# Batch 0's first norm inside attention's last steps, and batch 0 ahead of batch 1 up to the quantiser

## Chip, cores and metric

The kernel runs on one core of a Trainium2 chip. The metric is the device time of one execution in microseconds (us). Before the change it is 2540.73 us, the median of 3 runs (2538.59 to 2546.09).

## What is computed

Eight sequences of 512 tokens with 256 channels go through four layers. Cut to what matters here:

```
h = attention(x)                                  # 16 heads of 16, softmax, projection w_out
h = concat([cls_tok, h], axis=1)                  # T = 513 tokens
n = layernorm(layernorm(h)) * ln_w + ln_b         # the first norm, taken twice in a row
a = sigmoid(n @ W_alpha.T + b);  u = n @ W_B.T + b
s[t] = a[t] * s[t-1] + u[t]                       # recurrence over the tokens
h = h + s @ W_C.T + b + D * layernorm(h)
h = h + ffn0(layernorm(h))                        # the second norm; bit_linear: per token max,
                                                  # round(x * 127 / max), ternary weights;
                                                  # conv over 3 tokens; silu; bit_linear
h = h + mamba(layernorm(h));  h = h + ffn1(layernorm(h))
```

The two norms of the first layer share one variance: two roots, of (1+eps) var + eps^2 and of var + eps, give both scalings.

## The kernel before, in words

Activations lie with channels on partitions and tokens along the free dimension, 256 channels as two tiles of 128 x 513. A pair of sequences ("batch 0" and "batch 1", `p` = 0, 1) is worked at a time; four turns cover the eight. Each of the engines TensorE (PE), ScalarE (ACT), VectorE (DVE) and GpSimd (POOL) has its own instruction stream, written out by hand in the order of issue, and waits on counting semaphores; SyncE (SP) issues the DMAs. Nothing is reordered between streams by a planner.

**Attention** runs in 37 steps (`STEPS`), a head of either batch each. In step s TensorE makes four score tiles ("units", which rotate through PSUM banks 0 to 2 in the order of `plan_units`, and of which VectorE frees one at a time), four to six "shifted" score tiles of a head 8 steps back (L890), whose exponentials ScalarE takes (two tiles, 1024 columns, per activation, L1197), and at fixed steps the values product of a group of four heads (L902). A group's outputs are copied and shuffled (L1728, L1730), their sums inverted by ScalarE with Ln and Exp (`invert_sums`), and normalised by VectorE (L1737 to L1743) or GpSimd. Batch 0's projection stands in steps 29 and 30 (`O_STEP`), batch 1's behind the last step (L909), its last quarter behind four dummy matmuls (L762).

**Between attention and the first FFN** both batches go through each step together: `layer_norm(0)` (mean on TensorE by a matmul with 1/256, subtraction on VectorE L1577, square on ScalarE, variance on TensorE, Ln and Exp on ScalarE, product on VectorE L1583 and L1587), the affine on ScalarE, gates and inputs of the recurrence (weights `wa`, `wB`, L755), the scan on VectorE (L1786), its output product (`wC`), the residual (L1792, L1797), `layer_norm(2)`, the maximum over channels (`absmax`, L1591), per token maxima by transposes (L805, L1614), the scale spread as two rows "I" and "S" (L818), and the quantiser (L1644, L1524). ScalarE holds one table set at a time: Ln with Exp, Sigmoid, or Silu; a switch is an instruction of its own (L1201, L1300, L1317).

**The first FFN** is a loop over 2 x 8 tiles of 128 hidden channels: a fill on TensorE (L755), the scale by VectorE (L1813) or by ScalarE's copy and GpSimd (L2096), the convolution over tokens on TensorE for tiles 1, 2, 4 and 7 (L774) or as three taps on ScalarE and VectorE (L1819, L1825) for the others, Silu, and VectorE's maxima (L1596).

From the first norm on, every product of TensorE takes one of four PSUM slots in turn, in the order of `plan_fills`; a product waits until the reader of the slot's last content is done (`readers`). So the order of fills is also an order of waits. The functions are these:

## Time and profile before

| | |
|---|---|
| median of 3 runs | 2540.73 us |
| profiled execution | 2544.26 us, of which span 2542.4 us |
| turns | 4 |
| mean granted TensorE clock | 0.946 of full |

The profile is of one execution. PE's busy time is that of its matmuls, PEld's that of its weight loads, which overlap them. "x" counts instructions; a float32 matmul shows as two records. A line number is that of the kernel before; a helper's line (L755 for every fill, L1197 for every activation) is shared by many uses, so tile names and times tell them apart. In the timeline, instructions of one kind in a row are merged: the start is of the first, the us from the first start to the last end.

### The profile page before, as it was taken

The page shows a single profiled execution, that of the slowest core. Times are in us where ns is not written, and L with a number is a line of the kernel's source. Part 1 is how long each engine was busy: PE and PEld are TensorE (multiplying, and loading weights), DVE is VectorE, ACT ScalarE, POOL GpSimd, SP SyncE. Part 2 cuts the span into 40 slices and gives each one's busy share as a digit, 9 for nine tenths or more (in the row PEclk, how much of TensorE's full clock was granted, in tenths as well). Part 3 has the DMA queues.
Part 4 walks back from the last instruction along what each step waited for, and adds up shares of the span by engine and source line. Part 5 has one row for each costly group of instructions (what it writes and reads, how often), then busy time and mean ns, then how long its engine had stood idle before and what let it go on. Part 6 is the DMA issues. An engine that isn't in the chain of part 4 may idle for free.

```text
span 2542.4 us, 26885 instructions
## 1 busy us (share of the span) xinstructions
PE 2142.9 (84%) x9366; PEld 1193.9 (47%) x9366; DVE 2029.6 (80%) x2434; ACT 1488.5 (59%) x2363; POOL 1120.8 (44%) x562
## 2 busy tenths in 40 slices
PE   3998878897799887989779898788978988878897
PEld 1326664345423765434542476543553246644445
DVE  6865879997785588998788477999788747799977
ACT  2654468765275447875537544787453644577744
POOL 1220249982222115997222111799522311279952
PEclk8999999999899998999899998899989999889998
DMA  6200000000220000000031000000003100000000
GB/s 202 84 6 1 1 1 1 1 1 1 83 77 1 1 1 0 1 1 1 1 109 51 1 1 1 1 0 1 1 13 112 36 1 1 1 1 0 1 1 17
DMA packets 41087, 51.45 MB, mean 20 GB/s; under 512 B 9072, under 2 KB 32368, under 8 KB 40944
## 3 DMA queue, kind: packets, MB, share of 16 engines
q1 hardware_dynamic: 40944, 49.62, 6.3%
q8 instruction: 80, 1.31, 0.2%
q14 instruction: 63, 0.52, 0.1%
HBM read 26.25 MB, written 10.49 MB: 14 GB/s over the span
## 4 chain that ended last, share of the span: by engine, by line
DVE 40%; PE 39%; ACT 9%; issue 8%; POOL 3%; DMA 1%; SPq 1%; DVEq 0%; ACTq 0%; POOLq 0%
DVE big L1983 16%; PE psum L755 11%; PE psum L902 5%; ACT big L1197 4%; PE psum L818 3%; ACT mid L1197 3%; PE psum L890 3%; PE psum L875 3%; PE psum L1057 3%; DVE big L1652 2%; PE psum L1089 2%; POOL big L2132 2%; DVE mid L1596 2%; DVE negmax L1704 2%; DVE mid L1524 2%
## 5 line engine op out<-in xcount | busy, mean ns | idle before, releaser
L1197 ACT ACTIVATE big<-psum 128x512 f32<-128x512 f32 (+2 forms) x604 | 455.8, 774 | 277.3 <-PE psum L890 146.8
L2132 POOL TENSOR_TENSOR big<-big 128x2048 f32<-128x2048 f32 x124 | 561.8, 4530 | 41.3 <-DVE big L1983 41.2
L1057 PE MATMUL psum<-big,ident 128*128 128x512 f32 x992 | 507.0, 617 | 65.6 <-POOL big L2132 65.6
L1983 DVE TENSOR_TENSOR_SCAN big<-psum,b,big 128x512 f32<-128x512 f32 x404 | 490.2, 1265 | 6.9 <-ACT psum L1197 6.6
L1704 DVE TENSOR_REDUCE negmax<-psum 128x1 f32<-128x512 f32 x512 | 318.7, 678 | 47.2 <-PE psum L875 46.1
L1197 ACT ACTIVATE psum<-mid,aneg 128x512 f32<-128x512 f32 x404 | 268.5, 680 | 80.2 <-DVE big L1983 80.1
L1057 PEld LDWEIGHTS psum<-big,ident 128*128 128x128 f32 x992 | 174.4, 193 | 230.9 <-POOL big L2132 141.3
L875 PE MATMUL psum<-mid 96*128 96x512 bf16 x512 | 189.0, 389 | 49.3 <-DMA mid<-mid 38.1
L890 PE MATMUL psum<-mid 98*128 98x512 bf16 x512 | 182.2, 382 | 20.1 <-ACT big L1197 14.3
L1197 ACT ACTIVATE mid<-mid 128x513 f32<-128x513 f32 (+3 forms) x120 | 104.3, 883 | 154.7 <-DVE mid L1993 80.6
L2096 POOL TENSOR_TENSOR big<-big,mid 128x513 f32<-128x513 f32 x40 | 50.8, 1282 | 286.3 <-ACT big L1197 286.3
L2121 POOL TENSOR_TENSOR big<-mid,big 128x512 f32<-128x512 f32 (+1 forms) x128 | 154.8, 1209 | 19.9 <-ACT big L1197 19.9
L1197 ACT ACTIVATE mid<-psum 128x513 f32<-128x513 f32 (+1 forms) x100 | 59.3, 597 | 170.2 <-PE psum L818 139.3
L1927 DVE TENSOR_TENSOR big<-mid,psum 128x1024 f32<-128x1024 f32 (+1 forms) x128 | 157.5, 1230 | 0.1
L818 PE MATMUL psum<-ident,tok 128*128 128x128 f32 (+1 forms) x640 | 120.4, 340 | 33.3 <-DVE tok L1631 15.4
L902 PE MATMUL psum<-big,mid 128*32 128x512 f32 x1024 | 135.0, 627 | 10.6 <-ACT osb L1197 10.6
L1031 PE MATMUL psum<-bcp,sel 96*128 96x512 bf16 x256 | 101.8, 404 | 47.1 <-DVE big L1983 22.7
L1075 PEld LDWEIGHTS psum<-big 128*128 128x128 f32 x864 | 114.1, 193 | 57.7 <-issue 51.4
L1983 DVE TENSOR_TENSOR_SCAN big<-big,b,psum 128x512 f32<-128x512 f32 x108 | 135.6, 1256 | 3.9 <-ACT psum L1197 2.1
L1197 ACT ACTIVATE big<-ident,big 128x128 f32<-128x128 f32 x432 | 136.4, 386 | 0.0
L818 PEld LDWEIGHTS psum<-ident,tok 128*128 128x128 f32 (+1 forms) x640 | 108.8, 246 | 53.5 <-DVE tok L1631 21.1
L875 PEld LDWEIGHTS psum<-mid 96*128 96x128 bf16 x512 | 49.8, 98 | 178.0 <-DVE negmax L1704 85.1
(224 smaller groups left out, 3837.5 us busy)
## 6 DMA issues: line engine op xcount, KB each, us to landing
mid<-mid SPq DMA_DIRECT2D x192, 64.0 KB, 2.6
mid<-scratch SPq DMA_DIRECT2D x192, 64.0 KB, 2.2
scratch<-big SPq DMA_DIRECT2D x4, 1536.0 KB, 6.1
out<-hres SPq DMA_DIRECT2D x8, 513.0 KB, 5.0
big<-in_x SPq DMA_DIRECT2D x8, 512.0 KB, 5.5
big<-in_w SPq DMA_DIRECT2D x2, 1024.0 KB, 6.4
big<-in_wg SPq DMA_DIRECT2D x1, 1024.0 KB, 9.7
big<-in_wu SPq DMA_DIRECT2D x1, 1024.0 KB, 11.6
```

Source lines behind the costliest of these rows:

```text
L755: mm = nc.tensor.matmul(o[:, a:b], lhs, rhs[:, a:b], start=(n == 0), stop=(n == len(products) - 1))
L818: mm = nc.tensor.matmul(o[:, t0:t0 + n], tok[0:n, p, which, c:c + 1].broadcast_to([n, P]), ident[0:n, 0:n], start=True, stop=True)
L875: nc.tensor.matmul(unit(("S", h, t)), q_stack[0:ROWS_MAX, h % H, t * P:(t + 1) * P], k_stack[0:ROWS_MAX, h % H, :], start=True, stop=True) ...
L890: mm = nc.tensor.matmul(st_unit(v)[:, t % 2], k_stack[0:KROWS, h % H, t * P:(t + 1) * P], q_stack[0:KROWS, h % H, :], start=True, stop=True)
L902: mm = nc.tensor.matmul(pv_bank[32 * j:32 * j + 32, :], vaug[:, g // NG, t, HG * (g % NG) + j], probs[:, g % 2, j, t], start=(t == 0), sto ...
L1057: mm = nc.tensor.matmul(y_psum[:, c], ident[:, :], st(1, k)[:, c], start=(n == 0), stop=(n == NS - 1))
L1197: return nc.scalar.activation(o, a, func, **kw)
L1704: V.tensor_reduce(negmax[:, m % 2, k:k + 1], unit(("S", h, t)), AX_X, ALU.max, negate=True).then_inc(unit_free, 1)
L1927: V.tensor_tensor(st(0, k)[:, 0:m], mid4(k // NS, 3)[:, 0:m, 1:T], b_psum.unsqueeze(1).broadcast_to([P, m, S]), ALU.mult).then_inc(b_used, 1)
L1983: V.tensor_tensor_scan(st(0, k)[:, c], decays(DT * k + c), bx, b0[:, p, n, c:c + 1], ALU.mult, ALU.add).then_inc(scanned, 1)
L2121: G.tensor_tensor(st(0, k)[:, m:b_end(k)], mid4(k // NS, 3)[:, m:b_end(k), 1:T], b_row(k).unsqueeze(1).broadcast_to([P, b_end(k) - m, S]), ...
L2132: G.tensor_tensor(st(1, k), st(0, k), c_row(k).unsqueeze(1).broadcast_to([P, DT, S]), ALU.mult).then_inc(hc_ready, 1)
```

## The change

Batch 0's first norm moves into attention: mean behind step 31, square behind 32, variance behind 33, both roots behind 34, products behind 35, affine behind 36. Its mean and variance are taken in two halves of 257 and 256 tokens, as units in the banks of the scores. Batch 0's two gate fills come ahead of the last quarter of batch 1's projection, in place of the four dummy matmuls. From there batch 0 goes first through recurrence, second norm, maxima, token rows and quantiser, with batch 1's steps between them (`LRU_ORDER`), and batch 1's variance, transposes, token rows and quantiser stand inside the loop over FFN tiles (`AMONG`, `AT_R2`, `AT_N2`, `AT_T0`, `AT_I0`). The dummy matmuls ahead of the gates and ahead of the first transposes are gone. Two more switches of ScalarE's table set are made. The stacks of queries and keys lie group by group, and batch 0's norm writes over groups whose heads are done. The later norms' functions are only split up; their order is as before.

```
-WARM = {"affine": 20, "T0": 12, "I1_0": 10, "T1_1": 14, "I1_1": 6, "LN3": 8, "T2": 4, "T3_1": 14, "I3_1": 6}
-WARM_O = 4
+WARM = {"I1_0": 10, "T1_1": 14, "I1_1": 6, "LN3": 8, "T2": 4, "T3_1": 14, "I3_1": 6}
...
+LRU_ORDER = [("a0", 0), ("a1", 0), ("mean0", 1), ("u0", 0), ("u1", 0), ("var0", 1), ("c0", 0), ("c1", 0), ("a0", 1),
+             ("a1", 1), ("u0", 1), ("mean2", 0), ("u1", 1), ("var2", 0), ("c0", 1), ("c1", 1), ("T0", 0), ("I0", 0),
+             ("S0", 0), ("mean2", 1)]
+AMONG = {1: (("var2", 1),), 4: (("T0", 1),), 5: (("I0", 1), ("S0", 1))}
+AT_R2, AT_N2, AT_T0, AT_I0 = 2, 3, 5, 6
...
+MEAN_STEP, SQUARE_STEP, VAR_STEP, RSTD_STEP, NORM_STEP, AFFINE_STEP = (O_STEP + n for n in (2, 3, 4, 5, 6, 7))
...
+        if s == MEAN_STEP:
+            u.extend(("mean", n) for n in range(2))
+        if s == VAR_STEP:
+            u.extend(("var", n) for n in range(2))
...
-        q_stack = mb[:, 0:H * S].rearrange("p (h q) -> p h q", h=H)
-        k_stack = mb[:, H * S:2 * H * S].rearrange("p (h q) -> p h q", h=H)
+        stacks = mb[:, 0:2 * H * S].rearrange("p (j s h q) -> p j s h q", j=NG, s=2, h=HG)
...
+                def halves(key, stream):
+                    for n, (a, b) in enumerate(HALVES):
+                        unit_ready((key, n))
+                        for k in range(KT):
+                            mm = nc.tensor.matmul(unit((key, n))[:, 0:b - a], mean_w[:, :], stream[:, k, a:b],
+                                                  start=(k == 0), stop=(k == KT - 1))
+                        mm.then_inc(unit_full, 1)
...
+                    if s == MEAN_STEP:
+                        pe.wait_ge(cls_ready, 1)
+                        pe.wait_ge(unit_free, UNITS["O", 0, 1] + 1)
+                        halves("mean", hres[:, 0])
+                    if s == VAR_STEP:
+                        pe.wait_ge(squared0[0], 1)
+                        halves("var", mid2(0, 1))
...
-                        keep_busy(psum[:, spare * BANK:(spare + 1) * BANK], WARM_O)
+                        pe.wait_ge(probs_ready, 2 * HG * NGRP)
+                        pe.wait_ge(affine, KT)
+                        recurrence_inputs("a", wa, 0)
...
+                pe.wait_ge(cls_ready, PAIR)
+                mean(0, 1)
+                recurrence_inputs("u", wB, 0)
+                variance(0, 1)
+                recurrence_outputs(0)
+                pe.wait_ge(affine, 2 * KT)
+                recurrence_inputs("a", wa, 1)
+                recurrence_input("u0", wB, 1)
+                pe.wait_ge(h1_ready, KT)
+                mean(2, 0)
+                recurrence_input("u1", wB, 1)
+                variance(2, 0)
+                recurrence_outputs(1)
+                token_maxima(0, (0,))
+                token_rows(0, (0,))
+                pe.wait_ge(h1_ready, 2 * KT)
+                mean(2, 1)
                 for s in range(PAIR * HT + CONV_LAG):
+                    for part, b in AMONG.get(s, ()):
+                        if part[0] == "v":
+                            variance(2, b)
+                        elif part[0] == "T":
+                            token_maxima(0, (b,))
+                        elif part[0] == "I":
+                            token_rows(0, (b,))
...
+                def both_roots_first():
+                    one, two = mid1(0, 4), mid1(0, 5)
+                    for n, (a, b) in enumerate(HALVES):
+                        act.wait_ge(unit_full, UNITS["var", n] + 1)
+                        o = unit(("var", n))[:, 0:b - a]
+                        run(one[:, a:b], o, ACT.Ln, scale=1.0 + EPS, bias=eps_sq[:, 0:1]).then_inc(rstd0[0], 1)
+                        run(two[:, a:b], o, ACT.Ln, bias=eps[:, 0:1]).then_inc(unit_free, 1)
+                    act.wait_ge(rstd0[0], 2)
+                    run(one, one, ACT.Exp, scale=-0.5).then_inc(rstd0[0], 1)
+                    act.wait_ge(unit_free, UNITS["var", 1] + 1)
+                    run(two, two, ACT.Exp, scale=-0.5).then_inc(rstd0[0], 1)
+                def both_roots_second():
+                    wait_full(act, "var0", 1)
+                    for n, kw in enumerate((dict(scale=1.0 + EPS, bias=eps_sq[:, 0:1]), dict(bias=eps[:, 0:1]))):
+                        row = mid1(1, 14 + n)
+                        run(row, slot("var0", 1), ACT.Ln, **kw).then_inc(rstd0[1], 1)
+                        act.wait_ge(rstd0[1], 2 * n + 1)
+                        run(row, row, ACT.Exp, scale=-0.5).then_inc(rstd0[1], 1)
...
+                    if s == SQUARE_STEP:
+                        act.wait_ge(unit_free, UNITS["mean", 1] + 1)
+                        run(mid2(0, 1), mid2(0, 0), ACT.Square).then_inc(squared0[0], 1)
+                    if s == RSTD_STEP:
+                        both_roots_first()
+                    if s == AFFINE_STEP:
+                        affine_part(0)
                 invert_sums(NGRP - 1)
-                layer_norm(0)
                 nc.scalar.preload_act_table(ACT.Sigmoid)
-                for p in range(PAIR):
-                    act.wait_ge(ln_normed, q_of(0, p))
-                    for c in range(KT):
-                        run(mid2(p, 1)[:, c], mid2(p, 1)[:, c], ACT.Identity, bias=col("lnb", c),
-                                      scale=col("lnw", c)).then_inc(affine, 1)
                 act.wait_ge(pads, 4)
-                for p in range(PAIR):
-                    for c in range(KT):
-                        wait_full(act, f"a{c}", p)
-                        run(mid2(p, 3)[:, c, 1:T], slot(f"a{c}", p)[:, 1:T], ACT.Sigmoid, bias=col("ba", c)).then_inc(
-                            alpha_ready, 1)
-                    for c in range(KT):
-                        wait_full(act, f"u{c}", p)
-                        run(mid2(p, 4)[:, c], slot(f"u{c}", p), ACT.Identity, bias=col("bB", c)).then_inc(u_ready, 1)
+                gates(0)
                 load_ln_exp()
-                layer_norm(2)
-                nc.scalar.preload_act_table(ACT.Silu)
-                copy_rows(0)
+                act.wait_ge(centered0, 1)
+                run(mid2(1, 2), mid2(1, 0), ACT.Square).then_inc(squared0[1], 1)
+                for c in range(KT):
+                    gate_input(0, c)
+                both_roots_second()
+                nc.scalar.preload_act_table(ACT.Sigmoid)
+                affine_part(1)
+                gates(1)
+                load_ln_exp()
+                gate_input(1, 0)
+                squares(2, 0)
+                gate_input(1, 1)
+                log_variance(2, 0)
+                inverse_root(2, 0)
+                copy_rows(0, (0,))
+                squares(2, 1)
                 for s in range(PAIR * HT + 5):
+                    if s == AT_R2:
+                        log_variance(2, 1)
+                        inverse_root(2, 1)
+                        nc.scalar.preload_act_table(ACT.Silu)
+                    if s == AT_I0:
+                        copy_rows(0, (1,))
...
+                def normalise_first(p):
+                    dve.wait_ge(rstd0[p], 2 if p else 3)
+                    V.tensor_tensor(mid2(p, 1), mid2(p, 0), over_channels(mid1(p, 14 if p else 4)), ALU.mult).then_inc(
+                        normed0[p], 1)
+                    dve.wait_ge(rstd0[p], 4)
+                    V.tensor_tensor(mid2(p, 0), mid2(p, 0), over_channels(mid1(p, 15 if p else 5)), ALU.mult).then_inc(
+                        normed0[p], 1)
+                def centre_halves():
+                    for n, (a, b) in enumerate(HALVES):
+                        dve.wait_ge(unit_full, UNITS["mean", n] + 1)
+                        V.tensor_tensor(mid2(0, 0)[:, :, a:b], hres[:, 0, :, a:b],
+                                        unit(("mean", n))[:, 0:b - a].unsqueeze(1).broadcast_to([P, KT, b - a]),
+                                        ALU.subtract).then_inc(unit_free, 1)
...
+                    if s == MEAN_STEP:
+                        centre_halves()
+                    if s == NORM_STEP:
+                        normalise_first(0)
...
+                centre(0, 1)
+                recurrence(0)
+                normalise_first(1)
+                add_recurrence(0)
+                centre(2, 0)
+                recurrence(1)
+                norm_maxima(2, 0)
+                scales(0, 0)
+                add_recurrence(1)
+                quantise(0, 0, mid2(0, 0), mid2(0, 2), mid_bf(0, 1, 2))
+                centre(2, 1)
                 for s in range(PAIR * HT + 4):
+                    if s == AT_N2:
+                        norm_maxima(2, 1)
+                    if s == AT_T0:
+                        scales(0, 1)
+                    if s == AT_I0 + 1:
+                        quantise(0, 1, mid2(1, 0), mid2(1, 2), mid_bf(1, 1, 2))
```

## Rows read from the trace of the kernel before

**Rows 1.** The page, part 1: busy us (share of the span) and instructions.
```profile
PE 2142.9 (84%) x9366; PEld 1193.9 (47%) x9366; DVE 2029.6 (80%) x2434; ACT 1488.5 (59%) x2363; POOL 1120.8 (44%) x562
```
**Rows 2.** Windows, the FFN stage of turn 2: busy of each engine, clock, DMA.
```profile
875.00:917.00 42.00, 36.05 (x196) 28.76 (x194) 37.70 (x35) 22.27 (x37) 15.40 (x11) 0.96 0.00 1
```
**Rows 3.** Chain of waits, turn 2: start us, us, what.
```profile
814.33 2.01 PE psum L755 x8
...
816.36 1.24 DVE mid L1577
...
866.12 8.48 PE psum L818 x40
```
**Rows 4.** Timeline of TensorE, turn 2: start, us, line, shapes, [idle before <-releaser].
```profile
787.30 0.59 PE L890 MATMUL psum<-mid 98*128 98x512 bf16 x2 [0.55 <-ACT big L1197]
...
793.53 5.34 PE L902 MATMUL psum<-big,mid 128*32 128x512 f32 x32
...
802.78 3.64 PE L902 MATMUL psum<-big,mid 128*32 128x512 f32 x32
...
811.50 1.98 PE L909 MATMUL psum<-big,wo 128*128 128x512 f32 x4 [0.59 <-DVE big L1743]
...
843.26 7.09 PE L755 MATMUL psum<-mid,wC 128*128 128x257 f32 x32
...
874.53 2.57 PE L755 MATMUL psum<-mid,w 128*128 128x257 bf16 x20
877.56 2.83 PE L774 MATMUL psum<-big,onorm 128*128 128x257 f32 x12 [0.46 <-issue]
...
886.75 1.48 PE L755 MATMUL psum<-mid,w 128*128 128x257 bf16 x12
```
**Rows 5.** Timeline of VectorE, turn 2.
```profile
844.25 2.29 DVE L1786 TENSOR_TENSOR_SCAN mid<-mid 128x1026 f32<-128x1026 f32 x1 [4.63 <-ACT mid L1197]
846.47 1.39 DVE L1792 SCALAR_TENSOR_TENSOR hres<-psum,vec,hres 128x513 f32<-128x513 f32 x2
...
864.77 0.68 DVE L1614 TENSOR_REDUCE tok<-psum 128x4 f32<-128x512 f32 x1
...
875.14 0.70 DVE L1524 TENSOR_SCALAR mid<-mid 128x1026 bf16<-128x1026 f32 x1
...
887.46 0.69 DVE L1813 TENSOR_TENSOR big<-psum,mid 128x513 f32<-128x513 f32 x1 [0.62 <-PE psum L755]
```
**Rows 6.** Timeline of ScalarE, turn 2.
```profile
789.88 3.77 ACT L1197 ACTIVATE big<-psum 128x1024 f32<-128x1024 f32 x4 [1.80 <-PE psum L902]
...
820.77 0.69 ACT L1197 ACTIVATE mid<-psum,eps_sq 128x513 f32<-128x513 f32 x1 [0.36 <-PE psum L755]
...
825.27 1.15 ACT L1197 ACTIVATE mid<-mid 128x513 f32<-128x513 f32 x2
826.44 1.28 ACT L1300 ACT_TABLE_LOAD   x1
827.74 2.93 ACT L1197 ACTIVATE mid<-mid,vec 128x513 f32<-128x513 f32 x4
...
970.72 0.30 ACT L1197 ACTIVATE big<-psum 128x128 f32<-128x128 f32 x1
```
**Rows 7.** Windows of TensorE, turn 2: us, busy (records), granted clock, DMA share, GB/s.
```profile
790.00:793.00 3.00, 1.60 (x7) 1.00 0.01 1
793.50:797.00 3.50, 3.50 (x21) 0.56 0.00 0
909.00:912.00 3.00, 0.00 (x0) 1.00 0.00 0
914.00:920.00 6.00, 6.00 (x20) 0.50 0.01 3
```
**Rows 8.** Timeline of TensorE, token rows of turns 1 and 4.
```profile
243.96 5.65 PE L818 MATMUL psum<-ident,tok 128*128 128x128 f32 x40 [0.44 <-DVE tok L1631]
...
2115.57 9.95 PE L818 MATMUL psum<-ident,tok 128*128 128x128 f32 x40 [0.29 <-DVE tok L1631]
```

More of the change, by code:

```diff
@@ L132, in plan_fills @@
         order.extend((None, None, ("v0", p), ("v1", p)))
-    ln(0)
-    each("a0", "a1", "u0", "u1")
-    each("c0", "c1")
-    ln(2)
-    quantiser(0)
+    order.extend((None, None))
+    order.extend(LRU_ORDER)
     for s in range(PAIR * HT + CONV_LAG):
+        order.extend(AMONG.get(s, ()))
         if s < PAIR * HT:
@@ L1130, in mean4 @@
                     pe.wait_ge(h3_ready, 3 * p + 3)
[L1131 to L1135 removed]
+                    mean(4, p)
                 def project_last(c):
@@ new lines, in both_roots_second, with affine_part @@
+                def both_roots_second():
[5 more added lines that the diff above has]
+                        run(row, row, ACT.Exp, scale=-0.5).then_inc(rstd0[1], 1)
+                def affine_part(p):
+                    act.wait_ge(normed0[p], 1)
+                    for c in range(KT):
+                        run(mid2(p, 1)[:, c], mid2(p, 1)[:, c], ACT.Identity, bias=col("lnb", c),
+                            scale=col("lnw", c)).then_inc(affine, 1)
@@ L1257, in turn_functions, with gates, gate_input @@
+                def gates(p):
+                    for c in range(KT):
+                        wait_full(act, f"a{c}", p)
+                        run(mid2(p, 3)[:, c, 1:T], slot(f"a{c}", p)[:, 1:T], ACT.Sigmoid, bias=col("ba", c)).then_inc(
+                            alpha_ready, 1)
+                def gate_input(p, c):
+                    wait_full(act, f"u{c}", p)
+                    run(mid2(p, 4)[:, c], slot(f"u{c}", p), ACT.Identity, bias=col("bB", c)).then_inc(u_ready, 1)
                 copy_high(1)
```

222 lines of the change are left out of this document (98 added, 124 removed).

## Prediction

> **What bounds the kernel now.** I read the page first: VectorE is busy 80% of the span, TensorE 84%; neither is full, so hand-overs decide [rows 1]. The four turns are alike and I work in the second. Its windows say that the FFN stage is VectorE's, 37.70 of 42 us [rows 2]. The chain of waits before that stage goes through the mean, the centring, and on to 8.48 us of token rows: one engine at a time [rows 3]. So I read what the change is worth at one instant, the start of batch 1's first FFN fill, 886.75 (the first of three fills that the row merges, rows 4). VectorE takes it at 887.46 [rows 5] and is nearly full from there; all work behind it is the same in the same order, so a shift here reaches the end.
>
> **First stretch: attention's last steps.** Batch 0's norm goes between heads that TensorE and ScalarE already share.
> TensorE: a product of 8 records costs 1.73 us (7.09 us for 32, less the last's drain of 0.15, over four, rows 4). The mean starts at 786.60, where TensorE would idle to 787.30 [rows 4], and ends at 788.33, 1.03 us late. The values behind it and so ScalarE's next exponential move from 789.88 to 790.91 [rows 6]; the DMA of the last maxima moves as much and lands before it is wanted. The square is as wide as one of the four exponentials in that row (3.77 / 4, some 1.0 with its end); behind two of them it ends at 793.81. The variance runs 793.87 to 795.60, and the next heads' values start at 796.13 instead of 793.53: 2.60 late.
> Now a gain. These 32 value records took 5.34 us and the next 32 took 3.64 [rows 4]. The clock was granted at 0.56 during the first, after a stretch with TensorE busy 1.60 of 3 us [rows 7]. Mean and variance fill that hole; I take the fast price, 1.70 less, delay 0.90. If the clock still falls, that gain is nil.
> ScalarE takes both roots between two exponentials. Four Ln of about 257 columns have no row: from above 0.69, a Ln of 513; from below 0.30, an activation of 128 [rows 6]; between them by columns 0.43, or 0.38 in a row. Two Exp (1.15 for two, rows 6, and a wait of each on its input) make it 2.58. The last exponential is 3.49 late, the last values 3.09 (they had waited for a projection): 805.87 to 809.44, two projections to 813.08.
> Then both gate fills, 3.46 us, stand ahead of the last projection. It used to wait until 811.50, 5.1 behind the values [rows 4], for VectorE's copy, ScalarE's Ln and Exp and three steps more; now that is ready at 814.53, so 1.45 of 3.46 are covered. It starts at 816.54. **First term +5.04 us.** The affine (two of 2.93 / 4, rows 6) lies in ScalarE's wait for the last sums: nothing, 1.5 without that cover. GpSimd's taps start as much later and are wanted only by the first convolution: nothing. The new layout of the stacks moves the same bytes in as many DMAs: nothing, bounds 0.5 us either way.
>
> **Second stretch: to batch 1's scan.** The residual that the mean at 814.33 [rows 3] read is ready at 819.32. Mean 2.01 to its reader [rows 3]; behind it batch 0's input fills, 3.46; variance full at 826.60. ScalarE's four (0.69 and about 0.65 each) end at 829.22, the sigmoid load of 1.28 [rows 6] at 830.52, the affine at 832.04. Two gate fills and an input fill, batch 0's second mean at 837.29, the last input fill, full at 841.08. ScalarE has batch 0's square ahead of it and copies it by 842.26; scan 842.33 to 844.62. Before, it ended at 846.54 [rows 5]. **Second term −6.96**: 1.92 ahead, batch 0's recurrence and both its norms done beside it. Here the change gains.
>
> **Third stretch: to batch 1's maxima.** Now batch 0 stands in front. Behind the scan VectorE normalises batch 0 (1.24, as the centring, rows 3), takes its maxima (as long), waits for two fills and the transposes to 848.85, takes the scales (0.68 of reduction [rows 5] and four small ones, 1.35 to where the token rows start at 866.12 [rows 3], 0.2 for the last) and adds batch 1's recurrence only at 850.35 (two pairs of 1.39, rows 5, overlapping): 853.06, against 852.46. Mean, centring, square and variance: full at 859.60. ScalarE has an FFN copy ahead of Ln and Exp (861.76), then the Silu load (863.1), another copy and tile 0's product (864.4). VectorE has tile 0's tap queued ahead of the normalisation, and it waits for that product: tap to 865.2, normalisation 866.4, maxima 867.60. Before, maxima ended at 864.77 [rows 5]. **Third term +4.75**: 2.83 late.
>
> **Fourth stretch: to batch 1's first fill.** Before, 864.77 to 886.75 is 21.98 us, mostly both batches' token rows and batch 0's fills and convolutions. After, TensorE is idle from 860.7 to 867.65, and then has in its queue: batch 1's transposes (0.7), fill f4 (2.57 / 5), convolution 1 (2.83), batch 1's token rows (half of 5.65 at full clock, rows 4 and 8), fill f5. At full clock f5 is full at 874.95. ScalarE then copies f5, makes a product and a Silu, copies both rows, and reads convolution 1 (six of some 0.57, 3.4 us); only that read frees the PSUM slot that convolution 2 wants, at 878.5. **This is the new wait that I expect to rule.** Queued behind it are f6 and, on VectorE behind f6 (0.69) and a tap, batch 1's quantiser (1.24 and 0.70, rows 3 and 5): convolution 2 to 881.3, first fill of batch 1 at 885.1, 1.65 early.
> But the clock will not hold. After 3 us of idleness to 912 it was at 0.50 from 914 to 920, TensorE busy all the while [rows 7]; here the idleness is 7 us. A low spell between 3.5 and 6.8 us (the token rows of turn 4 ran cold over nearly all of 9.95, those of turn 1 in 5.65, rows 8) costs half its length, 1.7 to 3.4. A second is due at convolution 2, behind 3.7 us of idleness: 0.4 to 2.5 (5.3 for 2.8). First fill 887.2 to 891.0; I take 889.1. **Fourth term −0.48**, and the sum is +2.35.
> The other old turns are shorter by 0.36 on average, last projection to first fill, as their token rows ran from 5.65 to 9.95 [rows 8] against 8.48. So +2.7 a turn, **+10.8 us** in four. The profiled execution took 2544.26 us: 2555.1. The median of the runs is 3.53 lower: 2551.5, rounded down.
>
> **A rule against the change.** The rows: a table load took 1.28 us; it began 0.02 after the end of the activation before it, and the one behind it began 0.02 after its own end [rows 6]. The change makes five loads a turn of three. Two newly lie on the path, for sigmoid and for Silu, both in the terms; one has left it.
> The Trainium skill (ScalarE: Activation LUTs, "What ACT_TABLE_LOAD costs") adds to the load of about 1.28 us a drain of about 1.38 at every switch, and asks to do all of one set before the next. By that rule the estimate would be 1.4 us a turn more. These rows show no drain.
>
> **Rivals.**
> *The clock holds* (22%). TensorE stays at 1.00 through the queue behind batch 1's transposes. For: the token rows of turn 1 took 5.65 us after a pause of 2.25. Against: the pause is 7 us. It decides below 886.4 in the second turn, where the mean old turn stands. Price 885.1 − 886.4 = −1.3 a turn, −5 in all: 2535.5; with Ln at its lower bound (4 × 0.13 less) and the layout's 0.5 gained −2.3, 2531.5. This is the side of faster.
> *The first term is smaller* (12%): the affine and both roots fit where ScalarE waits for TensorE, 2.6 us less a turn: 2541.
> *Cold throughout* (13%): group 6's values stay slow (+1.7), batch 0's own rows run cold (2.8 more at most, 1.4 likely) and the spells are long (+1.9 less what overlaps): +3 a turn over mine, 2563.
> *A load drains* (3%): both on the path twice as long, by rows 2 × 1.28 × 4 = 10 more: 2561.
>
> **How the numbers follow.** My forecast has 50%, and its own range is 2544 to 2558. A measurement can tell about 0.3% from no change, 7.6 us: 2533.1 to 2548.3. Of my case 31% lies inside. Slower: 0.69 × 50 and 16, some 50%. Same: 0.31 × 50, 12 and 4 of the clock's case, 32%. Faster: its other 18. The range, 2533 to 2565, takes in most of the clock's case below and the cold one above.
>
> **What would show it.** Right: in turn 2, 28 us from the first shifts of step 32 to the last projection (24.2 before); 28 from there to the end of batch 1's scan (35 before); an idle TensorE of 6 to 7 us ahead of batch 1's transposes, and of 3 to 4 ahead of convolution 2, released by ScalarE; the clock near 0.5 behind each; group 6's values in 3.6. Wrong: no gap ahead of convolution 2; the first fill under 99 us behind those shifts; or the difference in another stage.

## Result, and the profile after

The kernel after takes 2566.89 us, the median of 4 runs (2562.72 to 2569.52), against 2541.45 before in 4 runs: ratio 1.0101, 95% interval 1.0083 to 1.0119. It is slower, the way the forecast leaned, but by 25 us where 11 were forecast, and it lies above the range. The profiled execution took 2567.67 us, 23.41 over that of before. Of all runs of this document one execution, of the kernel of the first experiment, was slow (5299.65 us); its ratio leaves it out, its median of 2547.08 does not (2546.62 without).

Part 1 of its page, as [rows 1]; TensorE has shed its dummy matmuls and nothing else stands out:

```profile
PE 2116.7 (82%) x9222; PEld 1181.6 (46%) x9222; DVE 2033.0 (79%) x2438; ACT 1499.7 (58%) x2379; POOL 1119.7 (44%) x562
```

TensorE's timeline in turn 2, as [rows 4]. The mean (L824) stands without a gap, the variance (L824 again, at 800.66) waits 0.34, and the 32 value records of the next group run in 3.64, not 5.34. Behind a wait of 1.05 us for ScalarE's roots a projection of four records took 3.63, where the same took 1.88 before (800.97):

```profile
793.42 1.90 PE L824 MATMUL psum<-hres,mean_w 128*128 128x257 f32 x8
...
795.68 1.92 PE L938 MATMUL psum<-big,mid 128*32 128x512 f32 x16
...
800.66 2.00 PE L824 MATMUL psum<-mid,mean_w 128*128 128x257 f32 x8 [0.34 <-ACT mid L1266]
...
803.02 3.64 PE L938 MATMUL psum<-big,mid 128*32 128x512 f32 x32
...
809.98 3.63 PE L945 MATMUL psum<-mid,wo 128*128 128x512 f32 x4 [1.05 <-ACT mid L1266]
...
824.11 1.88 PE L945 MATMUL psum<-big,wo 128*128 128x512 f32 x4
...
875.80 1.33 PE L841 MATMUL psum<-ident,mid 128*128 128x128 f32 x5 [7.26 <-DVE mid L1708]
...
877.78 4.74 PE L808 MATMUL psum<-big,onorm 128*128 128x257 f32 x12
882.36 2.75 PE L854 MATMUL psum<-ident,tok 128*128 128x128 f32 x20
...
889.22 4.22 PE L808 MATMUL psum<-big,onorm 128*128 128x257 f32 x12 [3.55 <-ACT big L1266]
...
898.16 1.49 PE L789 MATMUL psum<-mid,w 128*128 128x257 bf16 x12 [1.25 <-DVE mid L1631]
```

The two idle stretches of the forecast are there: 7.26 us ahead of batch 1's transposes, released by VectorE's maxima, and 3.55 ahead of convolution 2, released by ScalarE. The windows (as [rows 7]) show the granted clock with TensorE busy: full through the values of attention (first row), about half in that projection (second row) and in both stretches behind the idle ones (third and fourth rows; half is the level of 1.2 GHz). Columns: us, busy (records), clock, DMA share, GB/s:

```profile
793.50:797.00 3.50, 3.50 (x25) 1.00 0.00 0
809.98:813.54 3.56, 3.56 (x5) 0.52 0.02 5
875.80:882.00 6.20, 6.20 (x20) 0.52 0.01 3
889.00:893.00 4.00, 3.78 (x11) 0.62 0.00 0
```

The chain of waits over the same part (start us, us, what) shows what the 7.26 us consist of: copy, Ln, Exp, Silu load, two more ScalarE steps, tile 0's tap, normalisation, maxima. Then, behind the fill f5 (hidden tile 5, at 885.05), ScalarE works 3.4 us before convolution 2:

```profile
867.70 0.60 ACT big L1266
868.30 0.59 ACT mid L1266
...
868.91 0.63 ACT mid L1266
...
869.56 1.28 ACT L1427
...
870.85 1.31 ACT big L1266 x2
...
872.19 1.16 DVE big L1954
873.34 1.15 DVE mid L1688
...
874.51 1.25 DVE mid L1708
...
885.70 1.82 ACT big L1266 x3
887.52 0.98 ACT mid L1266 x2
888.50 0.59 ACT big L1266
...
889.22 4.22 PE psum L808 x12
```

Every turn, cut at six instants of these timelines (mean of the four turns, us). "Values" is the start of the 16 value records (795.68 above); the first four columns are the forecast's four stretches, each from the end of the one before; the last one runs from "values" to batch 0's second transposes, behind the FFN loop:

| kernel | values to last projection | to end of batch 1's scan | to batch 1's transposes | to batch 1's first fill | to second transposes | values to there |
|---|---|---|---|---|---|---|
| before | 23.64 | 35.47 | 18.36 | 21.06 | 19.05 | 117.59 |
| after | 27.97 | 27.94 | 24.17 | 23.16 | 19.06 | 122.30 |

The differences are the four terms of the forecast: +4.33, to which come the 1.03 that the mean delays the values, −7.53, +5.81 and +2.10; 5.74 a turn, 23.0 of the profiled 23.4. The FFN loop from batch 1's first fill on is unchanged. In turn 2 alone, the one that the forecast worked in, the terms are +5.8, −7.1, +5.4 and +0.5, 4.6 in all; the mean of the four is 0.8 us above turn 2's (122.30 against 121.54), since the clock fell at other places in each turn.

### The profile page after: what moved, and what is told of

Its sections match the earlier page's. It is cut to its first block, busy times and chain, and to the rows that moved or that the text cites. A ratio compares the mean times of both kernels' runs of the same rounds, so it can differ in the third digit from the quotient of the medians.

```text
span 2565.9 us, 26617 instructions
## 1 busy us (share of the span) xinstructions
PE 2116.7 (82%) x9222; PEld 1181.6 (46%) x9222; DVE 2033.0 (79%) x2438; ACT 1499.7 (58%) x2379; POOL 1119.7 (44%) x562
## 3 DMA queue, kind: packets, MB, share of 16 engines
q8 instruction: 78, 1.28, 0.2%
## 4 chain that ended last, share of the span: by engine, by line
DVE 41%; PE 38%; ACT 10%; issue 8%; POOL 2%; DMA 1%; SPq 1%; DVEq 0%; ACTq 0%; POOLq 0%
DVE big L2121 17%; PE psum L789 10%; ACT big L1266 5%; PE psum L938 5%; ACT mid L1266 4%; PE psum L911 3%; PE psum L926 3%; PE psum L854 2%; PE psum L1130 2%; PE psum L945 2%; PE psum L1162 2%; DVE big L1769 2%; DVE negmax L1821 2%; DVE mid L1631 2%; DVE big L2065 2%
## 5 line engine op out<-in xcount | busy, mean ns | idle before, releaser
L926 PE MATMUL psum<-mid 98*128 98x512 bf16 x512 | 181.7, 381 | 16.2 <-ACT big L1266 11.8
L2223 POOL TENSOR_TENSOR big<-big,mid 128x513 f32<-128x513 f32 x40 | 49.3, 1236 | 289.8 <-ACT big L1266 289.8
L1104 PE MATMUL psum<-bcp,sel 96*128 96x512 bf16 x256 | 102.2, 406 | 47.4 <-DVE big L2121 22.7
L938 PE MATMUL psum<-big,mid 128*32 128x512 f32 x1024 | 129.7, 604 | 11.4 <-ACT osb L1266 10.0
L854 PE MATMUL psum<-ident,tok 128*128 128x128 f32 (+1 forms) x640 | 105.3, 310 | 34.0 <-DVE tok L1748 19.7
L2273 POOL TENSOR_TENSOR big<-big,mid 128x513 f32<-128x513 f32 x40 | 49.4, 1239 | 172.5 <-ACT big L1266 172.5
```

The lines of the kernel that those rows point to most:

```text
L854: mm = nc.tensor.matmul(o[:, t0:t0 + n], tok[0:n, p, which, c:c + 1].broadcast_to([n, P]), ident[0:n, 0:n], start=True, stop=True)
L926: mm = nc.tensor.matmul(st_unit(v)[:, t % 2], k_stack(slice(0, KROWS), h % H)[:, t * P:(t + 1) * P], q_stack(slice(0, KROWS), h % H), star ...
L938: mm = nc.tensor.matmul(pv_bank[32 * j:32 * j + 32, :], vaug[:, g // NG, t, HG * (g % NG) + j], probs[:, g % 2, j, t], start=(t == 0), sto ...
```

## Experiments

Theory A: the order of batch 0 ahead of batch 1 costs, by the pause that it opens ahead of batch 1's transposes, by the wait that it makes at convolution 2 and by the cold clock behind both. The rivals stand in the expectations. All medians are of the same series as the ratio's kernel before (2542 to 2544 us). Stretches that are named without a profile line stand in the table at the end of this section. Each kernel has one profiled execution, so a single turn's clock is that of one execution.

**The clock.** Short dummy matmuls fill both pauses of the kernel after.

```
+ fill_gap("T0", 1, 56)          # ahead of token_maxima(0, (1,))
+ if p == 0 and c == 2: fill_gap("v4c", 0, 22)      # ahead of convolution 2
```

> The changed kernel with 56 dummy bf16 matmuls of 254 columns ahead of batch 1's transposes and 22 ahead of convolution 2, both in TensorE's idle time. Theory A (the two low spells of the clock are what I priced too low): the clock stays near 1.00 through transposes, f4, convolution 1, rows and convolution 2; in turn 2 transposes 0.71 instead of 1.33, convolution 1 2.8 instead of 4.7, convolution 2 2.8 instead of 4.2; batch 1's first fill 4 to 6 us earlier a turn, so 2543 to 2551 us. Theory B (the order of the queues alone sets the fill, the time won in the convolutions is waited out): the matmuls get short but the fill comes under 1 us earlier, 2563 to 2567.

Measured: 2547.08 us, ratio to before 1.0005 (0.9992 to 1.0018). The fourth stretch falls from 23.16 to 17.99 and nothing else moves. TensorE's timeline with the fillers (L797): the same work behind batch 1's transposes in 2.76 us a convolution. So 5.2 us a turn were the price of the clock.

```profile
866.43 6.24 PE L797 MATMUL psum<-w 128*128 128x254 bf16 x56 [0.39 <-ACT mid L1275]
...
874.36 2.76 PE L814 MATMUL psum<-big,onorm 128*128 128x257 f32 x12
...
883.72 2.87 PE L814 MATMUL psum<-big,onorm 128*128 128x257 f32 x12
```

**The wait of convolution 2.** Batch 1's token rows stand one step earlier, so that ScalarE copies them before it reads f5.

```
-AMONG = {1: (("var2", 1),), 4: (("T0", 1),), 5: (("I0", 1), ("S0", 1))}
-AT_T0, AT_I0 = 5, 6
+AMONG = {1: (("var2", 1),), 4: (("T0", 1), ("I0", 1), ("S0", 1))}
+AT_T0, AT_I0 = 4, 5
```

> The changed kernel with batch 1's token rows right behind its transposes, ahead of f4 and convolution 1, and its scales, row copies and quantiser one loop step earlier. Theory A (convolution 2 waits for ScalarE's row copies and the quantiser waits behind convolution 2): the idle time of 3.55 us ahead of convolution 2 goes, the quantiser no longer waits for f6, the first fill of batch 1 comes 4 to 6 us earlier a turn: 2543 to 2551 us. Theory B (the low clock takes it anyway, since the rows now run at half clock, 4.2 for 2.75): under 2 us a turn, 2559 to 2566.

Measured: 2547.76 us, ratio 1.0022 (1.0008 to 1.0036); the fourth stretch takes 18.71 us on average. The wait is gone and with it the second cold spell. The first is still there: the token rows, now in front, take 5.11 us in every turn, nearly twice their 2.75 at full clock, and the convolution behind them 4.36 in two turns and 3.02 and 3.25 in the others. In turn 1 the stretch took 17.98 all the same, as with the fillers: without the wait the queue has room for a part of the first spell. Moving one wait was worth 4.5 us, nearly as much as all the fillers.

```profile
874.72 5.11 PE L854 MATMUL psum<-ident,tok 128*128 128x128 f32 x20 [1.40 <-DVE tok L1748]
...
880.60 4.36 PE L808 MATMUL psum<-big,onorm 128*128 128x257 f32 x12
```

**The tap ahead of the normalisation.** Batch 1's normalisation and maxima stand ahead of tile 0's tap in VectorE's stream.

```
-AT_N2 = 3
+AT_N2 = 2
```

> The changed kernel with batch 1's normalisation and maxima one loop step earlier on VectorE, ahead of tile 0's tap. Theory A (third stretch: VectorE waits with the tap ahead of the normalisation): batch 1's transposes come 3.7 us earlier, the idle time ahead of them falls from 7.3 to 3.6, the low spell gets no longer; the first fill 3.5 to 5 us earlier a turn, 2547 to 2553 us. Theory B (the transposes are not what the fill waits for, since convolution 1 and f4 stand between): under 1 us a turn, 2563 to 2567.

Measured: 2544.34 us, ratio 1.0005 (0.9993 to 1.0017), a little better than theory A's range. The third stretch falls by 3.67 to 20.50, and the fourth by 1.60 to 21.56. The pause ahead of the transposes is 3.59 us and not 7.26; that the shorter pause is what shortened the cold spell is not shown, since below the same pause of 7.26 has spells of different length. VectorE's timeline: the normalisation starts right behind the root, where it used to wait for the Silu load, two ScalarE steps and the tap (873.26 in after, 869.54 the end of its root).

```profile
863.25 1.23 DVE L1688 TENSOR_TENSOR mid<-mid 128x1026 f32<-128x1026 f32 x1 [4.89 <-ACT mid L1266]
864.51 1.24 DVE L1708 TENSOR_REDUCE mid<-mid 128x513 f32<-128x1026 f32 x1
```

**The attention part without the order.** Second norm, maxima, token rows and quantiser of both batches together again, as before the change; first norm and gate fills inside attention as after it.

```
+ WARM "T0": 12;  AMONG = {}
- ... mean2(0) and var2(0) between batch 1's input fills, T0, I0, S0 by batch
+ mean2(0), mean2(1), var2(0), var2(1), T0 of both, I0 and S0 of both
```

> The attention part of the change alone: batch 0's first norm and gate fills in attention as changed, batch 0's recurrence ahead, but second norm, maxima, rows and quantiser of both batches together, as before the change, with the 12 dummy matmuls ahead of the transposes back. Theory A (the loss lies in the interleaving inside the FFN loop; the attention part costs 5.5 a turn at the last projection and gives back more by batch 1's scan): against the kernel before -1 to -4 us a turn, 2526 to 2538. Theory B (the attention part is what costs, and it is not given back): +4 to +6 a turn, 2557 to 2566.

Measured: 2518.72 us, ratio 0.9908 (0.9879 to 0.9936): faster than before and 48 us faster than after. Here the change's two parts come apart. The gain is in this half alone, and there is more of it than in the kernel after: batch 1's scan ends 2.2 us sooner behind the last projection. It is more than the forecast's best, 2526, and a part of it is the clock: of the 7.57 us a turn gained on before, 2.05 lie in the fourth stretch, which takes 19.01 here in every turn. The 48 us hold the clock too, since this kernel has its 12 dummy matmuls ahead of the transposes and the other none.

**The order without the attention part.** The counterpart.

```
- first norm, square, roots, affine of batch 0 in steps 31 to 36
+ ("mean0", 0), ("mean0", 1), ("var0", 0), ("var0", 1) ahead of the gates; the rest of LRU_ORDER and AMONG as after
```

> The other part alone: batch 0's first norm behind attention as in the kernel before, and batch 0 ahead of batch 1 through the recurrence, the second norm and its quantiser as in the kernel after. Theory A (the order costs, the attention part gains): group 5's values to the last projection as before, 23.6 us; batch 1's scan no earlier than before, 35.5 and up to 1 us more; the two stretches behind it as in the kernel after, 24.2 and 23.2, against 18.4 and 21.1: 8 us a turn more, ratio 1.012, some 2576, and no better than the kernel after. Theory B (the two parts need one another, and the order gains once batch 0's scan and norm are early): the scan of batch 1 comes 3 us or more earlier than before and the kernel is faster than the one after, under 2560.

Measured: 2607.96 us, ratio 1.0255 (1.0238 to 1.0272). Theory A's sign, twice its size: 17 us a turn. The miss is in the scan of batch 1, 45.8 us behind the last projection and not 36. Its chain of waits (turn 2) reads: fills of batch 0, its scan, then 13.45 us of fills in TensorE's queue that begin with batch 0's output product. Batch 1's gates stand behind a product that waits for batch 0's scan, and its scan behind batch 0's square on ScalarE. That product ran cold in three turns of four, 6.51 us in turn 2 against 3.73 in turn 4, and turn 4's stretch is 2.8 us shorter than turn 2's. In the kernel after, batch 0's gates stand in attention, ahead of all this. (This kernel keeps the dummy matmuls ahead of the gates and the last projection, as before; like the kernel after, it has none ahead of the transposes.)

```profile
847.38 7.21 PE psum L786 x32
...
855.40 2.30 DVE mid L1870
...
857.75 13.45 PE psum L786 x48
...
871.22 1.24 DVE mid L1657
...
872.48 1.65 ACT mid L1260 x2
...
874.22 2.31 DVE mid L1870
```

**The old kernel's own cold spell.** The kernel before, with 24 instead of 12 dummy matmuls ahead of its transposes.

```
-WARM "T0": 12
+WARM "T0": 24
```

> The kernel before, with 24 filler matmuls instead of 12 in the pause ahead of the token rows. Theory A (the clock's spell behind a pause of TensorE is what the fourth stretch costs, in the old kernel too where the pause outlasts its fillers): batch 1's transposes to its first FFN fill take 19.0 us in every turn, as in turn 1 of before, against 21.06 on average (19.01, 21.84, 20.08, 23.31); 2.0 us a turn less, 8 in all: ratio 0.9969, some 2536. Theory B (the spread between the turns is of other making): that stretch stays at 21 us on average and the time within 0.1% of before, or up to 1 us a turn more, if the added fillers outlast the pause and hold the transposes up.

Measured: 2530.92 us, ratio 0.9957 (0.9943 to 0.9971). The fourth stretch takes 19.02 in all four turns, against 19.01, 21.84, 20.08 and 23.31. The token rows of turn 4, 9.95 before [rows 8]:

```profile
2109.11 5.65 PE L818 MATMUL psum<-ident,tok 128*128 128x128 f32 x40 [0.45 <-DVE tok L1631]
```

The stretch gives 8.2 of the 14.9 us between the two profiled executions (11.8 between the medians). 3.4 more lie behind the FFN loop (47.42 us instead of 48.27 from the second transposes to the wbc product), where nothing was changed; the last experiment turns to it. So the stretch was cold in three turns of four before the change, and the kernel before is no warm baseline.

**Each pause by itself.** The fillers of the first experiment, in one pause at a time.

```
e11: fill_gap("T0", 1, 56) alone         e12: fill_gap("v4c", 0, 22) alone
```

> The kernel after with fillers in the first pause of TensorE alone, ahead of batch 1's transposes (56 of 254 columns), and none ahead of convolution 2. Theory A (each pause has its own cold spell and price: in turn 2 of after the queue behind the transposes took 2.9 us longer than with fillers, convolution 2 1.4, in the other turns up to 2.6): batch 1's transposes to its first FFN fill take 20.2 us, from 19.4 to 20.6, where both fillers gave 17.99 and none 23.16. Theory B (the second pause alone, 3.5 us, does no harm once TensorE was busy before it): 18.0 us, and the whole gain comes from the first fillers.

> The counterpart: fillers ahead of convolution 2 alone (22 of 254 columns), none ahead of the transposes. Theory A (separate prices): the stretch takes 20.9 us, 18.0 and the 2.9 of the first spell; the two single gains, 3.0 here and 2.3 there, add up to the 5.2 of both. Theory B (the spell of the first pause rules): it stays at 22.5 us or more, and the single gains do not add up.

Measured: 2556.21 us (ratio 1.0053, 1.0035 to 1.0072) and 2555.30 us (1.0055, 1.0038 to 1.0073); the fourth stretch takes 20.66 and 19.61. Both pauses have a price, so B falls in both. A's sizes (20.2, up to 20.6, and 20.9) are missed: the single gains are 2.50 and 3.55, 6.05 together, more than the 5.17 of both fillers. With the second pause filled, the first spell is shorter though nothing ahead of it changed within the turn: convolution 1 takes 3.16 us where it took 4.74. In turn 1, where nothing at all ahead of it differs, it takes 3.22 and in after 4.45, so this is a difference between two executions and no effect of the fillers. The medians, of six and nine executions, give 2.7 and 2.9 a turn, 5.6 together, and 5.0 for both fillers. With the first filled, all of convolution 2 is cold in three turns, as in the kernel after. The first row is of the second kernel, the next fence of the first.

```profile
875.91 3.16 PE L814 MATMUL psum<-big,onorm 128*128 128x257 f32 x12
```

```profile
883.89 5.47 PE L814 MATMUL psum<-big,onorm 128*128 128x257 f32 x12 [3.55 <-ACT big L1273]
```

What a spell costs was thus not constant for one and the same pause: over all turns of these kernels and of after it was 1.3 to 2.9 us at the first, and 1.4 to 3.0 at the second. What sets its length stays open.

**Tap and clock together.** The normalisation ahead of the tap, and fillers in both pauses (28 and 22).

```
AT_N2 = 2;  fill_gap("T0", 1, 28);  fill_gap("v4c", 0, 22)
```

> The kernel after, with batch 1's normalisation one tile earlier on VectorE and fillers in both pauses of TensorE (28 and 22 of 254 columns). Theory A (the third and the fourth term are two separate costs, a tap queued ahead of the normalisation and a cold clock): they add up; scan of batch 1 to its transposes 20.5 us as with the normalisation alone, its transposes to its first FFN fill 18.0 as with the fillers alone, against 24.17 and 23.16: 8.8 us a turn less than the kernel after, 35 in four, some 2531, ratio 0.9955 and so a little faster than before. Theory B (they are one cost: whoever takes away the pause takes the cold clock with it): no more than either alone, 5.2 us a turn, some 2546, ratio 1.001.

Measured: 2532.27 us, ratio 0.9959 (0.9944 to 0.9974). The third stretch takes 20.07 and the fourth 18.37; they add up. The change with its order kept is then faster than the kernel before, but not than that kernel with a warm clock.

**The gate fills out of attention's end.** From here the attention part alone is improved. Both of batch 0's gate fills go behind batch 1's variance. With them batch 0's scan and output product move beside batch 1's, and two table loads a turn go, so the edit is not one of place alone.

```
- pe.wait_ge(affine, KT); recurrence_inputs("a", wa, 0)    # ahead of the last projection
+ keep_busy(psum[:, 4 * BANK:5 * BANK], 4)
+ recurrence_inputs("a", wa, 0)                            # behind variance(0, 1)
```

> The attention part alone, as in the run before it, but both gate fills of batch 0 stand behind batch 1's first variance and not ahead of the last projection, so that one sigmoid load serves both batches. Theory A (2.0 us of the first term are the gate fills that the wait ahead of the last projection does not cover): group 5's values to the last projection take 26.4 us instead of 28.40, and the stretch to batch 1's scan stays at 25.7 (the fills fit where VectorE and ScalarE centre and square, and a load of 1.28 us goes): 2 us a turn less, ratio 0.988 with 1.2 either way, some 2511 where that run stood at 2519. Theory B (something else holds the last projection, and batch 0's early recurrence is worth its fills): the projection starts within 0.5 us of before, the scan of batch 1 ends 1 to 2 us later for the two scans in a row, and the time is that of the run before it or up to 8 us more.

Measured: 2506.78 us, ratio 0.9858 (0.9842 to 0.9875). Values to last projection 26.54 instead of 28.40, the stretch to the scan 26.26; 1.25 more came behind the scan, where the output product had been cold in three of four turns (5.42 us and 3.73).

**The roots behind the exponentials.**

```
- if s == RSTD_STEP: both_roots_first()
+ if s == RSTD_STEP + 1: both_roots_first()
- affine_part(0) in AFFINE_STEP;  + behind invert_sums(NGRP - 1)
+ values(*place) of the last heads ahead of batch 1's projection;  normalise_first(0) behind the last step
```

> The same, and both roots of batch 0 stand behind the last exponentials of attention (one step later), the values of the last heads ahead of the projections, the affine behind the last sums. Theory A (the other 2.6 us of the first term are the six small instructions of ScalarE between two exponentials): group 5's values to the last projection take 23.8 to 24.4 us, as in the kernel before (23.64) with 1.0 for the mean; some 0.5 of it comes back in the stretch to the scan: 2 us a turn less than the kernel with the gate fills moved, ratio about 0.985, some 2503. Theory B (the roots fitted where ScalarE waits for TensorE, and moving them costs cover): no difference over 0.5 us a turn, or up to 2 us a turn more, since the affine and the roots now stand in ScalarE's queue behind the last sums.

Measured: 2504.10 us, ratio 0.9845 (0.9829 to 0.9861); against the kernel without it only 2.7 us, no more than such medians spread. Values to last projection fall to 24.16 in three turns (27.30 in the first, where the variance and the last values ran cold), but 0.9 of 2.4 comes back before the scan, since the affine and the norm are late there. The 2.4 us are not the roots' price alone. Ahead of the move a projection waited 1.05 us for them, and in three turns of four TensorE's clock fell there or at the variance: the kernel with the gate fills moved takes 25.69 where all is warm, 26.55 or 27.37 where not. Warm against warm the move gives 1.5 us, and the place that the work moved to costs 0.9 of it; the rest is cold clock.

**The clock behind the FFN too.**

```
-WARM "I1_0": 10
+WARM "I1_0": 22
+ if f == 0 and p == 1: keep_busy(flat_slot(f"{name}0", p), 14)    # down-projection of batch 1
```

> The fastest kernel so far (attention part with the gate fills and roots moved), with fillers in two more pauses behind the FFN stage: 22 instead of 10 ahead of batch 0's token rows of the second quantiser, and 14 ahead of batch 1's down-projection. Theory A (the clock costs there too, as the old kernel with more fillers showed by chance: 47.42 us from batch 1's second transposes of that stage to the wbc product, against 48.27): that stretch takes 47.0 to 47.4 us in every turn instead of 48.9: 1.5 us a turn less, 6 in four, some 2498, ratio 0.982. Theory B (the pauses are VectorE's, and TensorE's clock isn't on the path): the stretch stays at 48.9, the time within 0.1%, or above by up to 1 us a turn where fillers outlast the pause.

Measured: 2496.92 us, ratio 0.9812 (0.9786 to 0.9838), the fastest kernel of all: 44 to 47 us under before. From the second transposes to the wbc product it takes 45.42 us, from 48.90; more of a gain than expected (47.0 to 47.4), while some stretches of attention run 1.7 slower (values to last projection 25.41). The token rows behind the added fillers:

```profile
893.54 2.86 PE L854 MATMUL psum<-ident,tok 128*128 128x128 f32 x20 [0.87 <-DVE tok L1750]
```

and in the kernel without them:

```profile
897.96 5.11 PE L854 MATMUL psum<-ident,tok 128*128 128x128 f32 x20 [3.43 <-DVE tok L1748]
```

The stretches of all kernels (columns as above):

| kernel | values to last projection | to scan | to transposes | to first fill | values to second transposes |
|---|---|---|---|---|---|
| both pauses filled | 27.96 | 27.95 | 24.18 | 17.99 | 117.14 |
| token rows earlier | 28.36 | 27.95 | 23.74 | 18.71 | 117.81 |
| normalisation ahead of tap | 28.18 | 27.94 | 20.50 | 21.56 | 117.24 |
| attention part alone | 28.40 | 25.75 | 17.82 | 19.01 | 110.02 |
| order alone | 23.23 | 45.78 | 24.82 | 21.67 | 134.56 |
| before, more fillers | 23.64 | 35.47 | 18.36 | 19.02 | 115.53 |
| first pause filled | 28.60 | 27.95 | 24.18 | 20.66 | 120.45 |
| second pause filled | 28.60 | 27.95 | 24.17 | 19.61 | 119.39 |
| tap and clock | 28.60 | 27.95 | 20.07 | 18.37 | 114.06 |
| gate fills later | 26.54 | 26.26 | 16.57 | 19.02 | 107.43 |
| roots later | 24.95 | 26.70 | 16.57 | 19.01 | 106.28 |
| clock behind the FFN | 25.41 | 27.55 | 16.57 | 19.01 | 107.59 |

## Why the prediction was wrong: the mechanism held, sizes failed

**What bounds, and the way of the shift: right.** The FFN loop behind the first fill is the same length, and the sum of shifts at that fill is the difference of the runs.

**First term, +5.04: right on average, in part by luck.** Measured +5.36. The variance filled the hole and the values took 3.64 [rows 4]; four Ln and two Exp took the 2.58 of the forecast to within 0.1 (the rows below; the prices written out, 4 × 0.38 and 1.15, add up to 2.67). But the average is of two turns at +4.9 and two at +5.8. In these two the projection that waits 1.05 us behind the roots ran cold (3.63 us at a clock of 0.52 in turn 2, 2.86 in turn 3, 1.96 in the others), and no term has that. Moving the gate fills gave 1.9 of the 2.01 that were called uncovered; moving the roots gave 1.5 of 2.58 where all is warm, and the 2.4 measured hold that cold projection.

```profile
808.16 0.47 ACT L1266 ACTIVATE mid<-psum,eps_sq 128x257 f32<-128x257 f32 x1
808.52 0.48 ACT L1266 ACTIVATE mid<-psum,eps 128x257 f32<-128x257 f32 x1
...
809.58 1.18 ACT L1266 ACTIVATE mid<-mid 128x513 f32<-128x513 f32 x2
```

**Second term, −6.96: right.** Measured −7.53 on average and −7.10 in turn 2; turn 1 of before was 1.7 us longer than the others.

**Third term, +4.75: right in mechanism, 1.06 too small.** The tap in front of the normalisation is shown by the kernel that swaps them. In turn 2 the stretch took 0.64 more than priced against before: the tap was priced 0.8 and took 1.16, the rest is hand-overs. In one turn of four it took 1.68 more, by the clock: batch 1's variance ran cold there, 3.51 us and not 2.00.

**Fourth term, −0.48: the step that failed, in size and sign.** It measured +2.10. "But the clock will not hold" was right, the idle 7 us, the idle 3.6 us and the wait of convolution 2 are there; three sizes were off:
- The cold clock was priced at 4.0 (889.1 against 885.1 all warm). It cost 5.17, by the kernel with both pauses filled. Cut at the start of f5, the first spell cost 2.4 to 2.9 us, 2.6 on average, where 2.55 was priced: right, though no row shows a low spell of 6.8 us, the upper end that was taken. **The second spell, at convolution 2, is the term that was mis-sized: 1.45, the middle of 0.4 to 2.5, was priced.** It cost that in turn 2, but 2.9 to 3.0 in the three others, where convolution 2 was cold throughout (5.47 us) and the fills behind it in part; 2.56 on average.
- The all-warm stretch was priced at 17.45 (867.65 to 885.1) and takes 17.99. The one large miss in it is batch 1's quantiser: 1.24 priced from [rows 3], 2.12 taken.
- The second turn was taken for the mean of the old ones, with 0.36 for the difference. In this stretch alone it was 0.78 above their mean (21.84 and 21.06). The 0.42 between is no loss of time: it comes back in the second term.

These are 1.17, 0.54 and 0.42 of the 2.2 between the term with that 0.36 (−0.12) and the measured +2.10. With the third term's 1.06, the first's 0.32 and the second's −0.57 they make the 3.0 us a turn, 12 in all, between forecast and profile. Some 2.0 of the 3.0 are cold clock: 1.17 in the two spells, and 0.4 each, on average over the turns, in the projection and in the variance.

**The rivals.** "The clock holds" is refuted by its own counterfactual: where it does hold, the kernel takes 2547.08, not 2535.5. "Cold throughout" was the nearest, at 2563, but for other reasons: neither group 6's values nor batch 0's own rows (2.86 us for 20 records) ran cold; the second spell was long, and the clock fell at two places that nobody had priced. "The first term is smaller" falls. "A load drains": the Silu load took 1.28 and the next instruction began 0.01 behind it, and so did the one behind the sigmoid load at 836.67 (1.28 us, next at 837.96), so there is no drain in the trace at either.

```profile
869.56 1.28 ACT L1427 ACT_TABLE_LOAD   x1
870.85 0.60 ACT L1266 ACTIVATE big<-psum 128x513 f32<-128x513 f32 x1
```

**The range** was built about the mean of each cold spell and let the whole cold case weigh 13%. The second spell at its long end, a warm stretch 0.5 longer, a tap and hand-overs 0.6 longer and two more places where the clock fell all point one way.

**What the forecast did not see** is that the two parts pull apart: the attention part is worth −25 us, 8 of them the clock of the fourth stretch, and the order +48 on top of it, some 17 of them (4.15 a turn) in that same stretch, where the kernel after has no dummy matmuls. The order without the attention part costs +65, so the two do not simply add. The forecast summed both and left the split to the experiments.

## What to carry to other kernels

Price the halves of a change apart, each as a kernel of its own: here one half lost 48 us over the gain of the other. A wait that moves an engine's work behind its neighbour's can be paid twice where it opens a pause of TensorE, once as the pause and again as the cold matmuls behind it; look for the queue order that takes the pause away before filling it with dummy matmuls, and compare pause by pause how long the old kernel's were warm, because its mean hides them. A short wait counts too: behind 1.05 us of idleness the same four records took 1.96 us in two turns and 2.86 and 3.63 in the others. Where work is put in front of a wait that already stands, check that what was behind it isn't what another engine is waiting for.

## What the runs showed of the hardware

**A VectorE operation with two wide operands, neither in PSUM, is longer beside a GpSimd one.** Batch 1's quantiser product took 2.12 us in every turn of the kernel after, with a GpSimd product running for the first 1.04 us of it; tile 0's tap took 1.16 with one running for its first 0.60, where others took 0.74. The lengthening, 0.90 and 0.42, is nearly what the GpSimd operation still had to run. One kernel takes the neighbour away: with the token rows earlier the same quantiser product meets no GpSimd operation and takes 1.22 (last fence), as batch 0's does. Operations that read an operand from PSUM were not longer: those of 512 columns took 0.75 us while a GpSimd product of 4.57 us ran beside them (346.72 and 345.85, turn 1), and such operations took 0.74 to 0.75 with none. The other rows are of turn 2 of the kernel after.

```profile
346.72 4.79 DVE L2012 SCALAR_TENSOR_TENSOR mid<-psum,vec,mid 128x512 f32<-128x512 f32 x6 [0.94 <-ACT mid L1266]
...
860.68 1.22 DVE L1761 TENSOR_TENSOR mid<-mid 128x1026 f32<-128x1026 f32 x1
...
872.19 1.16 DVE L1954 SCALAR_TENSOR_TENSOR big<-big,vec 128x512 f32<-128x512 f32 x1 [7.50 <-ACT big L1266]
...
876.26 0.74 DVE L1960 SCALAR_TENSOR_TENSOR big<-big,vec 128x512 f32<-128x512 f32 x1
...
895.25 2.12 DVE L1761 TENSOR_TENSOR mid<-mid 128x1026 f32<-128x1026 f32 x1
```

```profile
345.85 4.57 POOL L2233 TENSOR_TENSOR big<-mid,big 128x2052 f32<-128x2052 f32 x1 [35.63 <-DVE big L1631]
...
871.53 1.26 POOL L2223 TENSOR_TENSOR big<-big,mid 128x513 f32<-128x513 f32 x1 [1.99 <-ACT big L1266]
...
895.03 1.26 POOL L2223 TENSOR_TENSOR big<-big,mid 128x513 f32<-128x513 f32 x1 [7.56 <-ACT big L1266]
```

```profile
887.67 1.22 DVE L1761 TENSOR_TENSOR mid<-mid 128x1026 f32<-128x1026 f32 x1
```

**The length of a cold spell is not fixed by its pause.** Behind one pause of 7.26 us, with the same work, convolution 1 took 4.24 to 4.74 us in the four turns of after, and 3.16 to 3.22 in three turns of the kernel that fills only the later pause (4.23 in the fourth). Turn 1 of the two kernels is the same up to there and took 4.45 and 3.22.
